# Unread matrix products added at the head and the tail of each table update in a chunked recurrence (one core, float32)

## The reference, cut to what matters

```python
def step(carry, xs):
    cp, cm = carry
    k_t, v_t, q_t, a_t, th_t, e_t = xs
    g = jax.vmap(jax.grad(loss_fn))(cp, k_t, v_t)
    nm = jax.tree_util.tree_map(lambda m, gg: m * s(e_t) - s(th_t) * gg, cm, g)
    np_ = jax.tree_util.tree_map(lambda p, m: p * (1.0 - s(a_t)) + m, cp, nm)
    out_t = jax.vmap(_mlp, in_axes=(0, 0))(np_, q_t)
    return ((np_, nm), out_t)
```

## Time and profile before

| | us |
|---|---|
| median of 3 runs | 10934.41 (10927.46 to 10938.42) |
| the profiled execution's own time | 10920.32 |
| its span in the profile | 10918.5 |
| first and last update begin at | 2794.3 and 9424.7 |
| TensorE busy over the span | 9048.3 |
| VectorE busy over the span | 4914.1 |
| mean granted TensorE clock | 0.855 |

### The profile page before, as it was taken

The page is one execution under the profiler, slowest core; times in us unless marked ns, Lnnn a source line. Parts: engine busy times, 40 slices in busy tenths (PEclk is TensorE's granted clock), DMA queues, the critical chain, the costliest instruction groups (busy, mean ns, idle before and its releaser), DMA issues. The chain is left out here.

```text
span 10918.5 us, 371322 instructions
## 1 busy us (share of the span) xinstructions
PE 9048.3 (83%) x151474; PEld 5910.9 (54%) x151474; DVE 4914.1 (45%) x13031; ACT 2119.8 (19%) x4839; POOL 227.6 (2%) x184
## 2 busy tenths in 40 slices
PE   6799944325699999999999999999999999967777
PEld 2466621123466676666666666667667666642222
DVE  3444435447444434434344444443443444445555
ACT  0233312221111111111111111111111111113433
POOL 0000000001100000000000000000000000000000
PEclk8799965558698898898988988989889898888888
DMA  2000001426211111211121111222222222200000
GB/s 61 8 11 11 11 24 40 136 43 133 52 33 52 54 56 52 57 52 54 53 56 53 55 54 55 76 73 82 68 74 81 68 77 77 59 21 12 11 9 11
DMA packets 961784, 563.10 MB, mean 52 GB/s; under 512 B 376334, under 2 KB 956694, under 8 KB 959766
## 3 DMA queue, kind: packets, MB, share of 16 engines
q1 hardware_dynamic: 947990, 544.62, 18.4%
q0 software_dynamic: 13312, 12.57, 0.6%
HBM read 331.63 MB, written 188.08 MB: 48 GB/s over the span
## 5 line engine op out<-in xcount | busy, mean ns | idle before, releaser
L2373 PE MATMUL bank<-mv,hdiag 128*32 128x144 f32 x63744 | 2085.9, 289 | 9.5 <-DVE hdiag L2565 8.9
L2373 PEld LDWEIGHTS bank<-mv,hdiag 128*32 128x32 f32 x63744 | 1956.8, 111 | 94.7 <-DVE hdiag L2565 13.1
L2426 PE MATMUL bank<-mvt,ydiag 128*32 128x256 f32 x31872 | 1944.3, 381 | 0.1
L2426 PEld LDWEIGHTS bank<-mvt,ydiag 128*32 128x32 f32 x31872 | 1038.6, 110 | 570.0 <-issue 3.2
L2300 PE MATMUL bank<-hist,hdiag 32*128 32x256 f32 x2048 | 499.0, 669 | 217.3 <-DVE hdiag L2510 217.3
L2243 ACT ACTIVATE work<-work 128x128 f32<-128x128 f32 x498 | 154.3, 310 | 2219.7 <-DVE work L2555 2219.7
L431 PE MATMUL att_bank<-att_qa,att_ka 32*124 32x248 f32 x2048 | 580.3, 410 | 0.5 <-DVE att_qa L645 0.5
L421 PE MATMUL att_bank<-att_ka,att_qn 32*124 32x496 f32 x1024 | 574.2, 658 | 3.7 <-DVE att_mx L606 3.7
L606 DVE TENSOR_REDUCE att_mx<-att_bank 124x2 f32<-124x496 f32 x512 | 344.7, 674 | 486.6 <-PE att_bank L421 486.6
L2598 DVE TENSOR_TENSOR rep<-bank,ta 128x128 f32<-128x128 f32 x249 | 72.7, 292 | 1029.4 <-PE bank L2373 1029.4
L2313 PE MATMUL bank<-r_ident,mvt 128*128 128x128 f32 x2048 | 502.9, 427 | 39.3 <-DVE mvt L2528 39.3
(11 more groups left out here) (414 smaller groups left out, 10927.0 us busy)
## 6 DMA issues: line engine op xcount, KB each, us to landing
ring<-between_slopes SPq DMA_DIRECT2D x320, 512.0 KB, 4.1
baset<-between_base_old SPq DMA_DIRECT2D x265, 128.0 KB, 2.0
baset<-between_base SPq DMA_DIRECT2D x265, 128.0 KB, 2.2
between_base<-work SPq DMA_DIRECT2D x256, 128.0 KB
hist<-h SPq DMA_DIRECT2D x1992, 8.0 KB
hist<-y SPq DMA_DIRECT2D x1992, 2.0 KB
hist<-dl SPq DMA_DIRECT2D x1992, 8.0 KB
between_base_old<-bo SPq DMA_DIRECT2D x240, 128.0 KB
```

Source lines behind the costliest of these rows:

```text
L2373: mm = e.matmul(psP[32 * j:32 * j + 32, 0:MW], hdiag[:, hf, r, j, :], mv1[:, hf, r, j, :], start=(hf == 0 and r == 0), stop=(hf == 1 and r ...
L2426: mm = e.matmul(psBack[hf][32 * j:32 * j + 32, :], ydiag[:, n, j, :], both, start=(n == 0), stop=(n == 7))
```

## The change

Products whose results nobody reads are put on TensorE at three places of each chunk, all with the identity as the stationary operand and the whole of `yth` (128 partitions by 512 columns) as the moving one, into the bank `psC[0]`:

- 16 of them at the head, ahead of `new_terms(0)`, behind two waits that TensorE did not have there (VectorE and ScalarE have both ended the chunk before) and a `settled`, which is a no-operation that counts a semaphore;
- 3 of them behind the two products of `rep`, ahead of the wait for `d3c`; they wait for ScalarE's last copy of a turned slab, which reads the banks `psC`;
- 4 of them behind the product of `ones` with `d3`, ahead of the first `turn`.

None is put inside the loop over X.

```diff
+                    def kept_warm(out, n):
+
+                        for _ in range(n):
+                            e.matmul(out, ident[:, :], yth[:, :, :].rearrange("p a s -> p (a s)"), start=True, stop=True)
+
...
+                    e.wait_ge(V.sem, V.begun(c))
+                    e.wait_ge(A.sem, A.begun(c))
+                    settled(e, s_pe)
+                    kept_warm(psC[0], 16)
                     new_terms(0)
                     new_terms(1)
...
                     mm.then_inc(T.sem, 1)
+                    e.wait_ge(A.sem, A.upd(c, "c1511"))
+                    kept_warm(psC[0], 3)
                     e.wait_ge(V.sem, V.upd(c, "d3c"))
                     e.matmul(psH[:, 0:384], ones[:, :], d3.rearrange("p w q -> p (w q)"), start=True, stop=True).then_inc(T.sem, 1)
...
+                    kept_warm(psC[0], 4)
                     e.wait_ge(T.sem, T.upd(c, "cb"))
                     e.nop().then_inc(T.sem, T.gap("tra"))
                     turn(0, V.step(c, 0, "ha", 1))
```

## The result

| | before | after |
|---|---|---|
| median, us (runs of one session) | 10936.42 (10927.46 to 10948.70, 4) | 11056.82 (11052.07 to 11066.03, 4) |
| profiled execution | 10920.3 | 11052.07, span 11050.3 |

The ratio is 1.0110 with an interval of 1.0095 to 1.0125: 120 us slower, against 129 us forecast. In what follows, times inside an update are counted from GpSimd's first instruction of that update (line 2126), which stands some 0.6 us behind VectorE's last result of the chunk before.

What follows compares the result with a forecast made beforehand. TensorE at clock 0.50 was taken to bound the slab pipeline. Head +123 us, pipeline nothing and tail +6 us gave +129 us on a median of 10934.4, so 11063 us, range 10995 to 11130.

Steps and rivals of the forecast that it cites:

- Start: Head: delay from VectorE's end to the first unread product, between 0.3 and 3.4 us with TensorE's loop return, taken as 1.5.
- The 32 passes: Head: the 16 unread products, two passes each, were to take 13.8 us at clock 1.00.
- Rows 4: Earlier trace rows of 32 passes of 496 columns in 6.88 us, from which 0.43 us a pass was priced.
- The clock: Head: work lost when the clock falls in many updates before the products, taken as 1.7 us, bounds 0 and 3.4.
- new_terms: Head: new_terms(0) and (1), behind the unread products at clock 1.00, were to take about 1.1 us in place of 2.11.
- The tail: Unread products delay the d3 product 1.45 us and the turn 1.4 more; first step gains 2.35; net +6 us over 16 updates.
- the lower bound: Smallest loss: head with immediate start and no clock fall, +85 us, tail saving 1 us an update, −16: +69 us.
- the products hide: Rival, chance 0.01: at half the pass time 16 head products fit the idle time; −38 us, 10895 us.
- the clock holds at the head: Case within the forecast, chance 0.15: no clock fall and an immediate start at the head, +85 to +95 us, 11025 us.
- the head runs wholly at 0.50: Rival, chance 0.03: head products take 27.6 us at clock 0.50, +330 us in all, 11265 us.
- the pipeline stays at 1.00: Rival, chance 0.08: slab pipeline keeps full clock, about 21 us less an update against 7.5 more at the head; 10725 us.
- the nearly empty 6 us behind the head's products: Early pipeline: in the first 6.3 us TensorE works about 2 us, so the clock falls before the second slab pair.

Runs made afterwards that it cites:

- e1_head16: The changed kernel without its 7 unread products at the tail, the head's waits and 16 products kept: 11049.73 us, ratio 1.0117 to the kernel before.
- e2_tail34: The changed kernel without its head (waits, no-operation and 16 products), only the 3 and 4 at the tail: 10935.93 us, ratio 1.0012 to the kernel before.
- e3_waits: e1_head16 without its 16 unread products, so only the two waits and the no-operation at the head: 10930.65 us, ratio 1.0006 to the kernel before.
- e4_head8: e1_head16 with 8 unread products at the head in place of 16: 10937.23 us, ratio 1.0010 to the kernel before.
- e5_16_pipe2: The changed kernel plus 2 unread products ahead of slab 0's transposes and 2 in each pipeline wait for the next wy: 10757.64 us, ratio 0.9845.
- e9_order: e7_tuned with SyncE's queue reordered: first two base stores ahead of the slope stores, alt loads behind the last base store: 10553.25 us, ratio 0.9656.
- e11_order_first: e9_order without the unread products in the waits for wy, the two ahead of slab 0's transposes kept: 10777.31 us, ratio 0.9854.
- e12_first_only: The changed kernel plus only 2 unread products between new_terms(1) and slab 0's transposes: 10951.58 us, ratio 1.0032 to the kernel before.
- e8_nohead: e7_tuned without its 8 unread products at the head, the two waits kept: 10830.29 us, ratio 0.9905 to the kernel before.
- e7_tuned: e5_16_pipe2 with 8 products at the head, one and two at the tail, one in wy waits behind a from_last: 10826.71 us, ratio 0.9904.

## Why the prediction was right, and where its sizes were off

**The direction and the cause hold.** The head, not the tail, and there the products, not the waits: `e1_head16` against `e2_tail34` and `e3_waits`. The pipeline gained nothing because the clock fell ahead of its second pair of slabs, in all 16 updates, at 17 to 24 us. Slab 0 to slab 15 takes 68.2 us before and 68.3 after, on the mean of the 14 looped updates.

**The head's terms, for a looped update.** I took +7.5 us. The mean of the 14 is 16.56 us from GpSimd's first instruction to slab 0, against 10.05 before: +6.5. Term by term:

- Start: 1.5 us taken after VectorE's end. Measured 0.4 in chunks 1 and 9, where a loop begins, and 1.0 to 1.7 in the 12 others, 1.71 in the third update. So a return of the loop does show here, at somewhat less than the size taken.
- The 32 passes: 13.8 us taken, 13.97 in the row of the fourth update. Rows 4, with columns of another width, gave the price well.
- The clock: 1.7 us taken as a mean. It fell at the head in 7 of 14, and there cost 15.56 − 13.97 = 1.6 us in the third. The mean is about 0.9. This term, the mis-sized one, holds 0.8 of the 1.0 us by which the head was over-priced, and the start's mean of 1.2 us the rest: I had read the longer idle time as a fall in most of the updates.
- `new_terms`: 1.1 taken, 1.16 measured.

**The first and the last update.** +10.5 us (taken 9.9) and +7.9 (taken 8.2). The head's sum is 14 × 6.5 + 10.5 + 7.9 = 109.4 us, against 123.

**The tail.** From slab 15 (the second of its two first-pass instructions) to the product with `d3` it is 7.2 us in the third update and was 5.7 before: +1.5, and 1.1 to 2.5 in other updates, 1.45 taken. The turn is 2.9 us later (2.85 taken), the start of the steps 2.7 (2.7 taken), the 88 passes 2.32 us shorter (2.35 taken). On the mean of the 16 updates the start of the steps is 2.67 later and the passes 2.25 shorter: +0.42 an update, 7 us, against 6 forecast. `e2_tail34` has 11 us, with an interval of 3 to 23, for the tail alone, without the head.

**Sum.** 109 + 7 = 116 us, where the medians show 120. In the two profiled executions it is 107.4 + 4.8 = 112 us behind the first update's start, so the sum is good to some 4 us and not better. In the working of the range, the lower bound takes 15.2 − 10.6 = 4.6 us for a looped head as 5; with 4.6 it is 10998 us, and the range's lower end of 10995 leaves out no corner there, other than the prediction says.

**The rivals.** That the products hide was wrong for 16 and is right for 8 (`e4_head8`). That the clock holds at the head came in 7 of the 14 looped updates, but only 2 of these also had the immediate start, so its price did not. That the head runs wholly at 0.50 did not come: its longest group of unread passes is 17.0 us. That the pipeline stays at 1.00 did not come either, but its price was sized well: it was to save about 21 us an update. Between slab 0 and slab 15, on the mean of the looped updates, `e5_16_pipe2`, whose clock did stay, has 16.8 us less than before, with its own products among them, and `e9_order` 19.8. What I held against this rival, the nearly empty 6 us behind the head's products, was right in place, though not in full: the rest of the pipeline can keep the clock for a while in some updates (`e11_order_first`, `e12_first_only`), and I had not reckoned with that. For the rule that I weighed beside it ("TensorE: Matmul & The Clock Gate" of the Trainium skill, table "Why this matters for your kernels", drops tied to long gaps between bursts), this trace does not agree: the fall at 3736.9 came with no gap behind the unread products longer than the 2.13 us of the rows above.

**What stays open.** Why the clock holds in one update and falls in the next with the same instructions is not settled: their beginnings differ by fractions of a us, and no run varied that alone. In `e11_order_first` and `e12_first_only` updates of both kinds have an idle time of TensorE of 1.99 us early in the pipeline, so its length does not tell them apart. Nor is it shown why the pipeline before stays at 0.50 with TensorE busy for 66.64 of 72.20 us, while the same pipeline with one or two unread products in each wait rises to 1.00 (`e8_nohead`). Other numbers of products were not tried on top of `e9_order`, so it is the best of these kernels and not shown to be the best of its kind.

## What to carry to other kernels

Work that only keeps an engine's clock up costs what does not fit into the wait it is put in, so first measure the wait (here 8 products were free, and 16 cost 7 us an update). Put it into the holes of the stage that is bound by that engine, and not ahead of it: two products in each hole made the pipeline 16 to 17 us shorter, while those at the head bought nothing that could be told. When an engine has been made faster, read the DMA queue's order again, for the next wait may be one that was worth nothing before.

## What was not expected of the hardware

- The clock comes up inside the filled pipeline with no unread product at the head: in `e8_nohead` at 11 to 15 us in the looped updates, with slab 0 at 10 us. Only the two ahead of slab 0's transposes and those in the pipeline's waits are left there.
- The same instructions had two outcomes within one execution: TensorE held 1.00 for 47.70 us while busy for 37.82 of them in one update of `e11_order_first`, and fell 6.5 us behind slab 0 in another. The kernel with such updates also spreads: `e12_first_only` has 124 us from its lowest to its highest of 10 runs, `e11_order_first` 91 in 4, the change 14 in 4.
- A single stall of TensorE in mid-pipeline, 6.95 us long, came with 31 us at 0.50, though the unread products went on in them (`e7_tuned`, third update, 3692 to 3723):

```profile
3692.00:3723.00 31.00, 27.52 (x143) 16.11 (x144) 10.45 (x26) 11.06 (x30) 0.00 (x0) 0.50 0.30 90
```
